# Attention of a vision transformer layer: scores of a head pair in a 32-row tile, three PSUM banks at a time

## What is computed

```python
def _local_band(q, k, v, window):
    ...
    qk = jnp.einsum('bhsd,bhswd->bhsw', q_f, k_unf)
    out = jnp.einsum('bhsw,bhswd->bhsd', qk, v_unf)
    norm = jnp.clip(qk.sum(-1, keepdims=True), 1e-06, None)
    return out / norm
def _stride_band(q, k, v, stride):
    ...
    kv = jnp.einsum('bhsd,bhse->bhde', k_s, v_s)
    out = jnp.einsum('bhsd,bhde->bhse', q_f, kv)
    ...
out = wl * out_local + ws * out_stride + wg * out_global
```

## Time and profile before

| | us |
|---|---|
| median of 3 runs | 254.46 |
| lowest, highest | 253.57, 254.52 |
| span of the profiled execution, first to last instruction | 251.3 |
| TensorE busy in the span | 226.0 (90%) |
| VectorE busy | 141.4 (56%) |
| ScalarE busy | 111.2 (44%) |
| GpSimd busy | 71.6 (28%) |

### The profile page before, as it was taken

The page is one execution under the profiler, slowest core; times in us unless marked ns, Lnnn a source line. Parts: engine busy times, 40 slices in busy tenths (PEclk is TensorE's granted clock), DMA queues, the critical chain, the costliest instruction groups (busy, mean ns, idle before and its releaser), DMA issues.

```text
span 251.3 us, 5038 instructions
## 1 busy us (share of the span) xinstructions
PE 226.0 (90%) x1662; PEld 193.5 (77%) x1662; DVE 141.4 (56%) x422; ACT 111.2 (44%) x253; POOL 71.6 (28%) x87
## 2 busy tenths in 40 slices
PE   8979998898999999999989839879999999999930
PEld 8968896675777757676878719679999999999930
DVE  5353588696859578574656790557867324334100
ACT  2364847753323744535086870345334344243210
POOL 4013160832040502213036610003324224233240
PEclk9999999999999999999999956999999999999996
DMA  6999999999500000001014945522423323322213
GB/s 129 199 239 160 232 265 267 301 259 265 194 4 0 3 1 4 0 0 31 0 32 144 329 95 132 118 78 49 73 40 57 55 37 60 54 39 18 28 18 90
DMA packets 26261, 25.78 MB, mean 103 GB/s; under 512 B 4970, under 2 KB 23261, under 8 KB 26221
## 3 DMA queue, kind: packets, MB, share of 16 engines
q1 hardware_dynamic: 22333, 22.17, 35.3%
q0 software_dynamic: 3568, 2.64, 7.9%
q10 hardware_dynamic: 336, 0.66, 1.5%
HBM read 16.57 MB, written 7.77 MB: 97 GB/s over the span
## 4 chain that ended last, share of the span: by engine, by line
PE 66%; DVE 10%; DMA 9%; ACT 7%; issue 4%; SPq 1%; POOL 1%; another core or an unknown queue 0%; DVEq 0%; POOLq 0%; ACTq 0%
PE ps L1025 11%; PE ps L1002 11%; PE ps L825 6%; PE ps L738 6%; PE ps L567 5%; DMA sums<-ys,xs 5%; DMA wemb<-in_L_tok_W_emb 4%; PE ps L1014 3%; PE ps L598 3%; PE ps L701 3%; PE ps L572 2%; PE ps L734 2%; PE ps L811 2%; ACT w1hi L1573 1%; ACT w1hi L1574 1%
## 5 line engine op out<-in xcount | busy, mean ns | idle before, releaser
L1765 POOL DMA_INDIRECT sums<-ys,xs x17 | 26.3, 1546 | 73.5 <-ACT ys L1652 66.8
L1025 PE MATMUL ps<-w2s,hidT 128*128 x204 | 36.1, 327 | 1.1 <-DVE hidT L1448 0.8
L567 PE MATMUL ps<-ones 114*128 114x128 f32 x238 | 34.8, 301 | 1.1 <-DVE ones L1073 1.1
L1025 PEld LDWEIGHTS ps<-w2s,hidT 128*128 128x128 f32 x204 | 33.1, 189 | 2.1 <-issue 1.6
L567 PEld LDWEIGHTS ps<-ones 114*128 114x128 f32 x238 | 32.1, 213 | 2.1 <-DVE ones L1073 1.1
L1002 PE MATMUL ps<-w1hi,xhi 128*128 x68 | 24.4, 359 | 2.6 <-issue 1.3
L1427 DVE TENSOR_TENSOR xlo<-ps,xhi 128x128 fp32r<-128x128 f32 x17 | 5.0, 292 | 35.8 <-ACT xend L1645 35.8
L1652 ACT ACTIVATE ys<-ps,xs 128x192 f32<-128x192 f32 x17 | 7.2, 421 | 39.9 <-PE ps L1025 37.6
L1534 ACT ACTIVATE qlb<-ps,cst 96x228 f32<-96x228 f32 (+1 forms) x36 | 12.1, 425 | 17.2 <-PE ps L772 17.1
L825 PE MATMUL ps<-qlb,kT 96*114 96x342 f32 (+1 forms) x48 | 18.0, 457 | 1.7 <-DVE at L1219 1.1
L1219 DVE TENSOR_TENSOR at<-ps,cst 114x342 f32<-114x342 f32 (+1 forms) x24 | 11.3, 471 | 8.7 <-PE ps L825 8.3
(11 more groups left out here) (202 smaller groups left out, 462.5 us busy)
## 6 DMA issues: line engine op xcount, KB each, us to landing
w2s<-in_L_ffn_W SPq DMA_DIRECT2D x8, 576.0 KB
sent<-blank SPq DMA_DIRECT2D x1, 3977.0 KB, 31.6
w1s<-in_L_ffn_W SPq DMA_DIRECT2D x4, 768.0 KB, 17.2
xs<-sent SPq DMA_DIRECT2D x17, 96.0 KB, 2.0
w1s<-in_L_ffn_W SPq DMA_DIRECT2D x4, 384.0 KB, 18.6
w1hi<-w1hi SPq DMA_DIRECT2D x8, 192.0 KB, 3.0
ximg<-in_x SPq DMA_DIRECT2D x12, 96.0 KB, 7.8
w1s<-in_L_ffn_b SPq DMA_DIRECT2D x1, 792.0 KB
```

Of the source, the lines that this page charges most:

```text
L567: pe.matmul(bank[:, 0:128], ones[:], ones[:], start=True, stop=True)
L1025: last = pe.matmul(ps[6 + j % 2][:, 0:D], hidT[:, k, :], of_expert(w2s[:, :, k, :], expert), start=(k == 0), stop=(k == FCH - 1))
L1765: po.indirect_dma_start(sums, bass.IndirectOffsetOnAxis(ap=xs[:, j % NS, D + TAIL + 1:].bitcast(U32), axis=0), ys[:, j % 2, :], None, comp ...
```

## The change

`scores` has two calls a group instead of four, one a half. Each is three products, one a head pair: 32 rows of `kT` (partitions 32r to 32r+31) with two copies of the same rows of the queries (228 columns), into banks 4, 5 and 6. Only two masked copies of the queries are needed, one with the even heads and one with the odd (`parity`), so `spread` writes two instead of six. `windows` takes all three banks in one operation of 684 columns, also twice a group. `keys_values` does both halves at once side by side in bank 5 and `own_blocks` is two operations over 96 partitions, which write the zeros of `kvb` as well, so GpSimd no longer clears it. Banks 4 and 5 are now shared: the first scores of a group wait for `own_blocks` and for the key products of the group two on, the key sums wait for the `windows` of three groups before, `keys_values` for the last `windows` of the group before, `places` for all `windows` issued in its step. The order within a step is written out anew on TensorE and VectorE; `hold_clock_aside` is gone, and t = 8 has twice four `hold_clock` products. The core of the diff (left out: the constant `parity`, the counts of semaphores that follow from two calls for four, and the clearing on GpSimd):

```diff
...
@@ -163,7 +166,8 @@
         def sem(name):
             return ctx.enter_context(nc.semaphore(name))
-        ps = [ctx.enter_context(nc.psum_tensor(f"ps{i}", [128, 512], F32)) for i in range(8)]
+        psum = ctx.enter_context(nc.psum_tensor("ps", [128, 8, 512], F32))
+        ps = [psum[:, i, :] for i in range(8)]
         sb = pool(ctx)
...
@@ -243,7 +247,7 @@
         den = sb("den", [GTOK, 3, HEADS])
         qsc = sb("qsc", [GTOK, 2, 3, D])
         qgT = sb("qgT", [HALF, 2, 2, GTOK])
-        qlb = sb("qlb", [HALF, 2, 2, HH, GTOK])
+        qlb = sb("qlb", [HALF, 2, 2, 2, GTOK])
         kvb = sb("kvb", [HALF, 2, 2, 2 * PER, HALF])
         at = sb("at", [GTOK, 2, HEADS, GTOK])
...
@@ -749,6 +748,8 @@
                     pe.wait_ge(dv_key_sums, g)
                 else:
                     pe.wait_ge(ac_weights, 6)
+                if g >= 3:
+                    pe.wait_ge(dv_windows, 2 * (g - 2))
                 pe.matmul(ps[4][0:n, 0:D], band[:, 0:n], ktok[:, g % KS, :], start=True, stop=True)
                 pe.matmul(ps[4][0:n, D:2 * D], strided[0:n, 0:n], ktok[0:n, g % KS, :], start=True, stop=True).then_inc(pe_key_sums, 1)
...
@@ -800,31 +801,38 @@
                                      start=True, stop=True)
                 last.then_inc(pe_on_anchors, 1)
-            def keys_values(g, i):
+            def keys_values(g):
                 n = group(g)[1]
-                pe.wait_ge(gp_masked_values, 2 * g + i + 1)
-                if 2 * g + i >= 1:
-                    pe.wait_ge(dv_keys_values, 2 * g + i)
+                pe.wait_ge(gp_masked_values, 2 * (g + 1))
+                if g >= 1:
+                    pe.wait_ge(dv_windows, 2 * g)
+                for i in range(2):
+                    for r in range(PAIRS):
+                        c = i * HALF + r * TW
+                        last = pe.matmul(ps[5][TW * r:TW * (r + 1), i * KV:(i + 1) * KV], ktok[0:n, g % KS, c:c + TW],
+                                         vm[0:n, g % 2, i, r].rearrange("p k c -> p (k c)"), start=True, stop=True)
+                last.then_inc(pe_keys_values, 1)
+
+            def scores(g, i):
+
+                t0, n, _ = group(g)
+                if i == 0:
+                    pe.wait_ge(ac_keys_turned, g + 1)
+                    pe.wait_ge(ac_local_queries, g + 1)
+                    pe.wait_ge(dv_keys_values, g + 1)
+                    pe.wait_ge(dv_key_sums, min(g + 3, GROUPS))
+                    if g >= 4:
+                        pe.wait_ge(dv_places, g - 3)
+                    if g == 0:
+                        pe.wait_ge(dv_embedded, GROUPS)
+                else:
+                    pe.wait_ge(dv_windows, 2 * g + 1)
                 for r in range(PAIRS):
-                    c = i * HALF + r * TW
-                    last = pe.matmul(ps[5][TW * r:TW * (r + 1), 0:2 * PER * TW], ktok[0:n, g % KS, c:c + TW],
-                                     vm[0:n, g % 2, i, r].rearrange("p k c -> p (k c)"), start=True, stop=True)
-                last.then_inc(pe_keys_values, 1)
-
-            def scores(g, m):
-
-                t0, n, _ = group(g)
-                i = m // 2
-                pe.wait_ge(ac_keys_turned, g + 1)
-                pe.wait_ge(ac_local_queries, g + 1)
-                if 4 * g + m >= 1:
-                    pe.wait_ge(dv_windows, 4 * g + m)
-                else:
-                    pe.wait_ge(dv_embedded, GROUPS)
-                pe.matmul(ps[6][0:n, 0:3 * n], kT[:, g % 3, i, 0:n],
-                          qlb[:, g % 2, i, 3 * (m % 2):3 * (m % 2) + 3, 0:n],
-                          start=True, stop=True).then_inc(pe_scores, 1)
+                    rows = slice(TW * r, TW * (r + 1))
+                    last = pe.matmul(psum[0:n, 4 + r, 0:2 * n], kT[rows, g % 3, i, 0:n], qlb[rows, g % 2, i, :, 0:n],
+                                     start=True, stop=True)
+                last.then_inc(pe_scores, 1)
             def from_anchors(g):
...
@@ -860,7 +868,7 @@
                 t0, n, _ = group(g)
                 pe.wait_ge(dv_both, 2 * g + 1)
-                pe.wait_ge(dv_key_sums, GROUPS)
+                pe.wait_ge(dv_windows, 2 * min(g + 4, GROUPS))
                 if g >= 1:
                     pe.wait_ge(dv_places, g)
                 pe.matmul(ps[4][0:n, 0:E], before[0:n, 0:n], both[0:n, g, :], start=True, stop=False)
...
@@ -896,46 +904,44 @@
                     pe.wait_ge(wg_in, 32)
                 if 0 <= t - 3 < GROUPS:
                     through_anchors(t - 3)
-                for m in range(4):
-                    if t == 3 and m == 2:
-                        hold_clock_aside(ps[5], 10)
-                    if t == GROUPS + 2:
-                        if m == 0:
-                            pe.wait_ge(ac_keys_turned, GROUPS)
-                        hold_clock(ps[3], 3)
-                    if 0 <= t - 3 < GROUPS:
-                        if m % 2 == 0:
-                            keys_values(t - 3, m // 2)
-                        elif t < GROUPS + 2:
-                            hold_clock_aside(ps[5], 3)
-                        scores(t - 3, m)
-                    if m == 0 and t == 2:
-                        hold_clock(ps[5], 4)
-                    if m == 0 and 0 <= t - 1 < GROUPS:
-                        key_sums(t - 1)
-                        turn_keys(t - 1)
-                    if m == 0 and 1 <= t < 4:
-                        xhat_turn(t + 1)
-                    if m == 1 and 0 <= t - 2 < GROUPS:
-                        turn_queries(t - 2)
-                    if m == 1 and t == 3:
-                        xhat_turn(5)
-                    if m == 0 and t == GROUPS + 3:
-                        hold_clock(ps[3], 3)
-                    if m < 2 and 0 <= t - 4 < GROUPS:
-                        outputs(t - 4, m)
-                    if m == 0 and t == GROUPS + 3:
-                        hold_clock(ps[3], 1)
-                        x2_turn(GROUPS - 2)
-                        hold_clock(ps[3], 3)
-                        places(GROUPS - 3)
-                    if m == 2 and t == GROUPS + 4:
-                        hold_clock(ps[3], 8)
-                    if m == 2:
-                        if 0 <= t - 3 < GROUPS:
-                            from_anchors(t - 3)
-                        if t - 5 == GROUPS - 1 or 0 <= t - 5 < GROUPS - 2:
-                            x2_turn(t - 5)
+                    keys_values(t - 3)
+                if t == 2:
+                    hold_clock(ps[5], 4)
+                if 0 <= t - 1 < GROUPS:
+                    key_sums(t - 1)
+                    turn_keys(t - 1)
+                if 1 <= t < 4:
+                    xhat_turn(t + 1)
+                if t == GROUPS + 2:
+                    pe.wait_ge(ac_keys_turned, GROUPS)
+                    hold_clock(ps[3], 4)
+                if t == GROUPS + 3:
+                    hold_clock(ps[3], 3)
+                if 0 <= t - 4 < GROUPS:
+                    outputs(t - 4, 0)
+                if t == GROUPS + 3:
+                    hold_clock(ps[3], 1)
+                    x2_turn(GROUPS - 2)
+                    hold_clock(ps[3], 3)
+                    places(GROUPS - 3)
+                if 0 <= t - 3 < GROUPS:
+                    scores(t - 3, 0)
+                if 0 <= t - 2 < GROUPS:
+                    turn_queries(t - 2)
+                if t == 3:
+                    xhat_turn(5)
+                if 0 <= t - 4 < GROUPS:
+                    outputs(t - 4, 1)
+                if t == GROUPS + 4:
+                    hold_clock(ps[3], 8)
+                if 0 <= t - 3 < GROUPS:
+                    from_anchors(t - 3)
+                if t - 5 == GROUPS - 1 or 0 <= t - 5 < GROUPS - 2:
+                    x2_turn(t - 5)
+                if t == GROUPS + 2:
+                    hold_clock(ps[3], 4)
+                if 0 <= t - 3 < GROUPS:
+                    scores(t - 3, 1)
                 if t >= GROUPS + 3:
                     hold_clock(ps[3], 1)
                 if 0 <= t - 5 < GROUPS:
...
@@ -1196,29 +1202,28 @@
                                      ps[0][0:HA, i * GTOK:i * GTOK + n].rearrange("p (b s) -> p b s", s=SEQ),
                                      r[:, i, :].unsqueeze(2).broadcast_to([HA, imgs, SEQ]), ALU.mult).then_inc(dv_anchored, 1)
-            def own_blocks(g, i):
-
-                imgs = group(g)[2]
+            def own_blocks(g):
+
                 if g >= 2:
                     ve.wait_ge(pe_heads, g - 1)
-                else:
-                    ve.wait_ge(gp_blocks_zero, 1)
-                ve.wait_ge(pe_keys_values, 2 * g + i + 1)
-                for r in range(PAIRS):
-                    c = slice(TW * r, TW * (r + 1))
+                ve.wait_ge(pe_keys_values, g + 1)
+                for i in range(2):
                     last = ve.tensor_tensor(
-                        kvb[c, g % 2, i, :, c].rearrange("p (k b) c -> p k b c", b=PER)[:, :, 0:imgs],
```

(70 more changed lines are left out.)

23 lines of the change are left out of this document (11 added, 12 removed).

## The result

The changed kernel takes 265.51 us (median of 4 executions, 259.80 to 281.15) beside 254.49 (253.57 to 269.16) for the kernel before. Both spread widely from one execution to the next, the longer ones at a lower mean clock, so ratios here leave those out of both kernels: the time over that of before is 1.0227, 95% interval [1.0114, 1.0339]. Forecast was 242.0, range 238.0 to 248.5, faster. It is slower, by 1.1 to 3.4%. The profiled execution has a span of 259.9 us, 8.6 more than before, at a mean clock of 0.867 where before had 0.971.

The account below looks back on a forecast made before the run. TensorE bounds loop steps t = 3 to 8 until VectorE becomes later; step gains sum to 13.1 us, less 0.6 for hops, 12.5: span 251.3 becomes 238.8, plus 3.2 gives 242.0 us, range 238.0 to 248.5.

Parts of the forecast that it names:

- What bounds the steps at full clock: Loop t = 3 to 8: TensorE bounds the steps until VectorE becomes the later one; TensorE alone would give 3.3 us at t = 5.
- the walk: Step-by-step timing of TensorE and VectorE with waits, t = 3 to 8: gains of 1.6 to 2.7 us each, sum 13.1.
- The prices: Costs per piece: score set 0.70 us (0.53 to 0.86), both `keys_values` halves 0.78, `windows` 0.87, own blocks 1.46.
- From span to time: Whole kernel: span 251.3 becomes 238.8 us, and 3.2 us is added to give the time, 242.0.
- Fillers: TensorE: `hold_clock_aside` removed, two times 0.77 us in t = 4 to 7, sixteen products in t = 3; 0.9 us at t = 8.
- Rival 1: Clock falls in t = 3 after TensorE idles 3.05 us; costs 2.8 + 0.4 us, giving 245.2; chance 0.16.
- Rival 3: Slower: holes without fillers hold TensorE at 1.2 GHz from t = 3 on, 293 us; decides from 12.5 us; chance 0.07.
- Chances: Whole forecast: own case 0.52, rivals 0.16, 0.14, 0.07 and 0.09, no change 0.02; faster by more than 0.5% 0.91, slower 0.07.

Follow-up runs that it names:

- the filled version: Changed kernel with plain fillers at TensorE's waits in t = 3 to 8, in t = 9, 10 and ahead of the last output biases: 243.19 us, ratio 0.9495.
- the first run: Changed kernel with plain fillers put back in t = 3 alone, 13 before the first scores and 6 before the second: 258.77 us, ratio 1.0061.

## Why the prediction was wrong, point by point

- **What bounds the steps at full clock, and the walk: right.** Step lengths at clock 1.00, forecast against the filled version: 12.75 and 13.06 at t = 5, 12.1 and 12.85 at t = 6, 10.3 and 10.69 at t = 7, 11.55 and 12.04 at t = 4, a gain of 1.7 and 1.4 at t = 3. Sum of gains 13.1 forecast, 10.35 with fillers in. Each step misses by 0.3 to 0.8 us, t = 6 most; without fillers and at full clock t = 6 was still 0.6 long in the changed kernel. In t = 4 the 0.31 us wait for ScalarE's `qx`, which the walk leaves out, is as long as that step's miss without fillers: 11.85 us for 11.55. The other way, TensorE's wait before the first scores was 0.20 to 0.27 us in t = 4 to 6 for 0.6 walked.
- **The prices: right.** A score set took 0.58 us (0.53 to 0.86 given, 0.70 taken), both halves of `keys_values` 0.82 (0.78), `windows` 0.87 (0.87), both own blocks 1.42 to their end (1.46). The Trainium skill's rule in "TensorE: Matmul & The Clock Gate", Part 3, on products in different row groups running at once had pointed at 0.53 for the set; the 0.58 here agrees.
- **From span to time: 1.4 us too much.** The forecast added 3.2 us, a median less the span of another execution. In each execution on record the time is 1.7 to 2.0 us over its own span, so the walk's own sum comes to 240.6.
- **Fillers: the step that failed.** The sum took two times 0.77 us a step of t = 4 to 7, and sixteen products in t = 3, as pure gain and put what they did for the clock at nothing. Taking them out alone, in the old kernel, costs 10.8 us between the fastest executions and 18.3 between the medians, where I had booked a gain. The walk then assumed a granted clock of 1.00 in all six steps; it was 0.72, 0.81, 1.00, 0.99, 0.50 and 0.77. I used clock 1.00 in the earlier trace rows, with the fillers in place, as evidence that steps 80 to 90% busy would hold it. For t = 4 and 5 that was so (three runs have no fillers in them and clock 1.00); t = 6, busy 10.92 of 12.69 us, ended in a fall.
- **Rival 1 had the mechanism and the place, with the price too low.** The fall at t = 3 came where told, after 3.12 us idle. I priced it from one return in the earlier trace rows, 5.6 us; it lasted 13.7, and cost 14.85 - 12.42 = 2.4 us in t = 3 and 14.05 - 11.85 = 2.2 in t = 4 (that step's length in the first run), 4.6 for 3.2.
- **Rival 3 had the result, slower, but not the form.** I asked for the clock to stay low from t = 3 on and put the point of decision at 12.5 us of work. It came back between, and fell twice more. By steps, against the filled version: t = 7 17.46 - 10.69 = 6.8 us, t = 8 2.1, and behind it, from 133.20 to the end 126.7 us against 119.0, 7.7. With 4.6 that is 21.2 us lost, against 12.2 gained (10.35 in the steps and 2.9 behind them in the filled version, less 1.0 by which t = 3 began later than before): 9 slower, and the span is 8.6 longer. These are differences of the same spans, so they have to close. That the loss is the clock is shown by where it lies, in the stretches under 1.00, and by the fillers, which add work and yet take the loss away. The share behind t = 8 is less clean, since the filled version has 26 more filler products there, and the 1.0 us ahead of t = 3 is not explained.
- **Chances.** 0.16 and 0.07 for two forms of one cause was too little for a change that takes all 40 column-tiled fillers off an engine whose clock falls and returns in the earlier trace rows, and the range had no case of several falls.

What stays open: which of the three things at the end of t = 6 and 7 matters (the two waits, or the thin products between them) was not separated, beyond the one fall that came before the second wait. Why the same kernel with the same waits keeps its clock in one execution and loses it in another is open, and why a low stretch lasts 3.4 us in one place and 55 in another while TensorE is busy throughout is not explained either.
